# Edge counts kept in PSUM per 16 targets, 480-wide one-hots from two tensors, and four stages rearranged

## What is computed

```python
feat_all = einsum('ni,rhid->rnhd', x, conv_weights)      # layer 0: attention over 8 relations, 4 heads
h = segment_sum(alpha * feat_all[type8, src], dst)       # alpha: softmax of leaky_relu(el + er) per dst
agg = segment_sum(relu-MLP_r(x)[src], dst)               # layer 1: 2 relations, gates, 3 small products
aggr = segment_sum(relu(x @ Wp + bp)[src], dst) / cnt    # layer 2: SAGE, twice
out = rows of xt gathered by dst, weighted by softmax over heads    # layer 3: first 1875 edges only
```

## Time and profile before

| | us |
|---|---|
| runs | 2119.39, 2126.85, 2128.66 |
| median | 2126.85 |
| the profiled execution, its own time | 2116.86 |
| its span, first to last instruction | 2115.1 |
[...]
| PE busy | 1475.9 |
| DVE busy | 1249.3 |
| ACT busy | 666.2 |
| POOL busy | 543.2 |

### The profile page before, as it was taken

One profiled execution on the slowest core, in us unless ns is written; L12 is line 12 of the kernel. 1 busy time (PEld: TensorE's weight loads), 2 busy tenths in 40 slices (PEclk: granted clock), 3 DMA queues, 4 the chain that ended last, 5 costly groups with the idle time before them and its releaser, 6 DMA issues.

```text
span 2115.1 us, 20437 instructions
## 1 busy us (share of the span) xinstructions
PE 1475.9 (70%) x5426; PEld 764.4 (36%) x5426; DVE 1249.3 (59%) x2926; ACT 666.2 (31%) x1118; POOL 543.2 (26%) x517
## 2 busy tenths in 40 slices
PE   6598988677766565304777775989976589889630
PEld 3254654111111111103555554544433254644520
DVE  5221222889998888687666676520036677576705
ACT  1024764677665555200000000357732110010010
POOL 0003774677777777300000000000000000000031
PEclk9797556555555555555999998989987579999865
DMA  5924664465565565502677772000000000000021
GB/s 197 64 106 152 195 208 132 128 196 182 182 197 185 191 195 184 159 0 91 192 207 207 204 208 86 1 22 1 1 1 0 30 1 1 1 1 2 10 65 49
DMA packets 98133, 223.84 MB, mean 106 GB/s; under 512 B 32984, under 2 KB 57476, under 8 KB 97540
## 3 DMA queue, kind: packets, MB, share of 16 engines
q1 hardware_dynamic: 74084, 158.00, 23.8%
q0 software_dynamic: 23968, 64.77, 11.6%
HBM read 140.09 MB, written 82.63 MB: 105 GB/s over the span
## 4 chain that ended last, share of the span: by engine, by line
PE 48%; DVE 21%; issue 12%; POOL 12%; DMA 3%; DVEq 2%; ACT 1%; SPq 1%; POOLq 0%; ACTq 0%
PE bank L1580 14%; POOL arena L497 10%; PE bank L1519 10%; PE bank L1397 5%; DVE adjacency L936 5%; PE bank L1430 3%; PE bank L1416 3%; DVE arena L1193 2%; DVE arena L1001 2%; PE bank L1646 2%; PE bank L1564 1%; PE bank L1643 1%; SPq L363 1%; PE bank L1548 1%; DVE arena L930 1%
## 5 line engine op out<-in xcount | busy, mean ns | idle before, releaser
L497 POOL DMA_INDIRECT arena<-feat_table,arena x469 | 506.8, 1081 | 300.0 <-issue 138.3
L1467 PE MATMUL bank<-arena 128*128 128x480 f16 x586 | 319.6, 565 | 176.2 <-DVE arena L930 125.2
L565 ACT ACTIVATE arena<-bank 128x480 uint16<-128x480 f32 x586 | 307.9, 586 | 85.1 <-PE bank L1467 82.7
L505 POOL DMA_INDIRECT arena<-al_table,edge_ends x15 | 14.1, 942 | 1168.0 <-DMA al_table<-arena 1163.7
L1580 PE MATMUL bank<-arena 128*128 128x472 f16 x1440 | 294.3, 368 | 9.9 <-DVE arena L1151 5.9
L1519 PE MATMUL bank<-arena 128*128 x966 | 225.9, 387 | 83.1 <-issue 83.0
L936 DVE TENSOR_TENSOR adjacency<-adjacency,arena 128x480 uint16 x586 | 234.9, 401 | 23.4 <-ACT arena L565 16.7
L1519 PEld LDWEIGHTS bank<-arena 128*128 128x128 f32 x966 | 180.1, 191 | 129.2 <-issue 106.7
L1467 PEld LDWEIGHTS bank<-arena 128*128 128x128 f16 x586 | 60.7, 104 | 435.2 <-DVE arena L930 272.0
L930 DVE TENSOR_SCALAR arena<-iota,arena 128x480 f16<-128x480 f16 x586 | 201.5, 344 | 0.0
L1580 PEld LDWEIGHTS bank<-arena 128*128 128x128 bf16 x1440 | 142.6, 99 | 161.7 <-issue 15.5
(11 more groups left out here) (273 smaller groups left out, 1565.7 us busy)
## 6 DMA issues: line engine op xcount, KB each, us to landing
edge_rows<-arena SPq DMA_DIRECT2D x67, 910.0 KB, 4.1
arena<-edge_rows SPq DMA_DIRECT2D x117, 520.0 KB, 4.0
feat_table<-arena SPq DMA_DIRECT2D x60, 256.0 KB, 2.3
arena<-feat_table,arena POOLq DMA_INDIRECT x469
arena<-in_w SPq DMA_DIRECT2D x1, 2048.0 KB, 9.7
arena<-in_xT SPq DMA_DIRECT2D x1, 1920.0 KB, 18.5
arena<-in_x SPq DMA_DIRECT2D x1, 1792.0 KB
xt_table<-arena SPq DMA_DIRECT2D x3, 528.0 KB, 3.3
```

Of the source, the lines that this page charges most:

```text
L497: g.indirect_dma_start(out=SLOT[k][:, j, :], out_offset=None, in_=feat_t, in_offset=bass.IndirectOffsetOnAxis(ap=IE[:, GB * b + j:GB * b + ...
L565: a.activation(EV[st % AS].rearrange("p r k -> p (r k)"), PS[4 + st % 4][:, 0:R2 * KW], ACT.Copy)\
L1467: mm(PS[4 + st % 4][:, 0:R2 * KW], OHS[st % AS], OHK[st % AS], start=True, stop=True).then_inc(s["a_mm"], 1)
```

## The change

In the walk the two one-hots are made by `tensor_tensor` instead of `tensor_scalar`: the 480-wide one compares an fp16 iota with one fp32 key column that is repeated along the row (`column_of`), the 128-wide ones are made for eight steps at once (`rows_of`). PSUM counts are no longer started anew per step: four banks are cleared once, window w adds into bank w mod 4, and the matmul's output address comes from a register. ACT copies, in every step, the bank of the window before the current one straight into ADJ at that window's offset; both addresses come from registers, loaded 16 + 16 at a time from a 16-bit table, and each copy waits for the one before. As banks are never cleared again, a window's copy holds the sum of every fourth window up to it; 29 subtractions after the walk undo this. Zeroing of ADJ and DVE's adds are gone. PE may be three steps ahead of ACT, not four.

Around it: the row sums load their 16 + 16 offsets in one load per 16 steps; counts per target are made during the first aggregation, after ADJ's two relations are added together; layer 2 casts that sum on ACT; the gates' products of a chunk are issued before the x products of the chunk before it, bank by bank; the tail runs in four groups of up to four tiles, each with its own semaphore, with its own Exp, Sqrt and normalisation.

```diff
-GC_FIRST, GC_ER = 4, 14
+GC_FIRST, GC_ER, GC_LATE = 4, 14, 0
...
+RK = 2 * RG
+RKG = -(-RSTEPS // RK)
...
+        OHK = [AR[:, A_OH + k * KW:A_OH + (k + 1) * KW].bitcast(F16) for k in range(AS)]
+        OHS = [AR[:, o:o + AS * P // 2].bitcast(F16).rearrange("p (k e) -> p k e", e=P) for o in (A_OH + AS * KW, A_OHB)]
+        PBANK = AR[:, A_PBK:A_PBK + STRIDE // 2].bitcast(U16)
+        ETABf = AR[:, A_ETB:A_ETB + STRIDE].bitcast(U16)
+        ETAB = ETABf.rearrange("p (g two s) -> p g two s", two=2, s=16)
+        Z16 = AR[:, A_Z16:A_Z16 + KW].bitcast(F16)
...
-            def zero(lo, hi):
-                return a.activation(EARLY[:, lo:hi], ones[:, 0:1].to_broadcast([P, hi - lo]), ACT.Copy, scale=0.0)
...
-                zero(ZW * g, ZW * (g + 1))
                 if g >= GC_FIRST and g % 2 == 0:
                     collect((g - GC_FIRST) // 2)
-            act.wait_ge(s["er_mm"], NG)
-            zero(Z0, ZN).then_inc(s["a_add"], 1)
...
-            def a_evac(i, st):
-                act.wait_ge(s["a_mm"], i * AU + (st + 1))
-                a.activation(EV[st % AS].rearrange("p r k -> p (r k)"), PS[4 + st % 4][:, 0:R2 * KW], ACT.Copy)\
+            def a_evac(st, bank, off):
+                act.wait_ge(s["a_mm"], max(st, 1))
+                if st:
+                    act.wait_ge(s["a_ev"], st)
+                a.activation(ADJ[:, :, bass.ds(off, KW)], BANKS[:, bass.ds(bank, R2 * KW)].rearrange("p (r k) -> p r k", r=R2), ACT.Copy)\
                  .then_inc(s["a_ev"], 1)
-            for st in range(AS):
-                a_evac(0, st)
             got = GC_ER
-            for n in range(A_N):
-                for u in range(AU):
-                    a_evac(n, AS + u)
-                    due = GC_ER + (NGB - 1 - GC_ER) * (AU * n + u + 1) // (A_N * AU)
-                    while got < due:
-                        collect(got)
-                        got += 1
...
+            for st in range(STEPS):
+                if st % 16 == 0:
+                    both_ = offsets(ACTE, 2 * st, 32, KW * (WINS - 1), ETABf)
...
+                    offs = both_[16:32]
+                a_evac(st, banks[st % 16], offs[st % 16])
+                due = min(GC_ER + (NGB - 1 - GC_ER - GC_LATE) * (st + 1 - AS) // (STEPS - AS), NGB)
+                while got < due:
+                    collect(got)
+                    got += 1
+            a_evac(STEPS, 512 * (4 + (WINS - 1) % 4), KW * (WINS - 1))
...
+                    def cast(c):
+                        if c >= 2:
+                            act.wait_ge(s["chunk_used"], (R2 + v) * SH + c - 1)
+                        a.activation(chunk(CH2, c % 2, wide), ADJ[:, 0, :].rearrange("p (n s) -> p n s", s=SH)[:, :, c],
+                                     ACT.Copy).then_inc(s["chunk_ready"], 1)
                     for t in range(NT):
                         act.wait_ge(s["p_mm"], NT * v + t + 1)
                         message(t, t % 4, wide)
+                        if t in (6, 10):
+                            cast((t - 6) // 4)
+                    for c in range(2, SH):
+                        cast(c)
...
-            act.wait_ge(s["s3_ready"], 1)
-            a.activation(S3[:, 0, :], S3[:, 0, :], ACT.Exp).then_inc(s["s3_exp"], 1)
-            ln_sqrt(4)
+            for q, (t0, t1) in enumerate(GROUPS):
+                act.wait_ge(s["s3_ready"], q + 1)
+                a.activation(S3[:, 0, H * t0:H * t1], S3[:, 0, H * t0:H * t1], ACT.Exp).then_inc(s["s3_exp"], 1)
+                act.wait_ge(s["var_ready"], 3 + q + 1)
+                a.activation(RS[:, t0:t1], MV[:, t0:t1, 1], ACT.Sqrt).then_inc(s["std_ready"], 1)
...
+            W1 = slice(0, 1)
+            v.memset(ETABf[W1], 0)
+            v.tensor_copy(WCUR[W1], WS[W1])
+            link(v.tensor_scalar(WPRE[W1], WS[W1], 3.0, None, ALU.add))
+            v.tensor_single_scalar(WCUR[W1], WCUR[W1], 3, ALU.bitwise_and)
+            link(v.tensor_single_scalar(WPRE[W1], WPRE[W1], 3, ALU.bitwise_and))
+            def by_16(j, values, m, b):
+                full = STEPS // 16
+                v.tensor_scalar(ETAB[W1, 0:full, j, :], values[W1, 0:16 * full].rearrange("p (g s) -> p g s", s=16), m, b, ALU.mult, ALU.add)
+                v.tensor_scalar(ETAB[W1, full, j, 0:STEPS - 16 * full], values[W1, 16 * full:STEPS], m, b, ALU.mult, ALU.add)
+            by_16(0, WPRE, 512.0, 2048.0)
+            link(v.tensor_scalar(WS[W1], WS[W1], -1.0, 0.0, ALU.add, ALU.max))
+            v.tensor_scalar(PBANK[W1, 0:STEPS], WCUR[W1], 512.0, 2048.0, ALU.mult, ALU.add)
+            v.memset(Z16, 0.0)
+            by_16(1, WS, float(KW), 0.0)
...
-            def onehots(st, lo, key):
-                v.tensor_scalar(OHS[st % AS], iota128[:, :], lo, None, ALU.is_equal)
-                v.tensor_scalar(OHK[st % AS], iota480[:, :], key, None, ALU.is_equal).then_inc(s["a_oh"], 1)
-            def add_step(i, st, off):
-                dve.wait_ge(s["a_ev"], i * AU + (st + 1))
-                dve.wait_ge(s["a_add"], i * AU + (st + 1))
-                dst = ADJ[:, :, bass.ds(off, KW)]
-                v.tensor_tensor(dst, dst, EV[st % AS], ALU.add).then_inc(s["a_add"], 1)
-            dve.wait_ge(s["a_add"], 1)
...
+            def rows_of(st, n, lo):
+                v.tensor_tensor(OHS[st // AS % 2][:, 0:n, :], iota128[:, :].rearrange("p (a j) -> p a j", a=1).to_broadcast([P, n, P]),
+                                lo.rearrange("p (s a) -> p s a", a=1).to_broadcast([P, n, P]), ALU.is_equal).then_inc(s["a_rows"], 1)
+            def column_of(st, key):
+                v.tensor_tensor(OHK[st % AS], iota480[:, :], key.to_broadcast([P, R2 * KW]), ALU.is_equal).then_inc(s["a_oh"], 1)
+            rows_of(0, AS, SLO[:, 0:AS])
             for st in range(AS):
-                onehots(st, *step_cols(st))
+                column_of(st, KEY[:, st:st + 1])
+            dve.wait_ge(s["et_mm"], SC)
             with dve.Fori(0, A_N) as i:
-                offs = offsets(DVE, i * AU, AU, KW * (WINS - 1))
                 dve.wait_ge(s["a_oh"], i * AU + AS)
                 v.tensor_copy(SK, SLO_KEY[:, :, bass.ds(i * AU + AS, AU)]).then_inc(s["turn_cols"], 1)
                 dve.wait_ge(s["turn_cols"], i + 1)
                 for u in range(AU):
-                    add_step(i, u, offs[u])
-                    onehots(AS + u, SK[:, 0, u:u + 1], SK[:, 1, u:u + 1])
...
+                    dve.wait_ge(s["a_mm"], i * AU + (u + 1))
+                    if u % AS == 0:
+                        rows_of(AS + u, AS, SK[:, 0, u:u + AS])
+                    column_of(AS + u, SK[:, 1, u:u + 1])
+            for st in range(AS + A_N * AU, STEPS):
+                dve.wait_ge(s["a_mm"], st - AS + 1)
+                if st % AS == 0:
+                    rows_of(st, STEPS - st, SLO[:, st:STEPS])
+                column_of(st, KEY[:, st:st + 1])
+            dve.wait_ge(s["a_ev"], STEPS + 1)
+            for lo in range((WINS - 1) // 4 * 4 * KW, 0, -4 * KW):
+                n = min(4 * KW, WINS * KW - lo)
+                link(v.tensor_tensor(ADJ[:, :, lo:lo + n], ADJ[:, :, lo:lo + n], ADJ[:, :, lo - 4 * KW:lo - 4 * KW + n], ALU.subtract))
...
+            dve.wait_ge(s["chunk_ready"], SH)
+            link(v.tensor_tensor(ADJ[:, 0, :], ADJ[:, 0, :], ADJ[:, 1, :], ALU.add))
+            link(v.tensor_reduce(CNTX, ADJ[:, 0, :].rearrange("p (n s) -> p n s", s=SH), AX.X, ALU.add))
+            dve.wait_ge(s["chunk_used"], R2 * SH)
+            v.tensor_copy(CNTS, CNTX).then_inc(s["cnt_red"], 1)
...
-                n0, n1 = CQ * c, min(CQ * (c + 1), NW)
-                v.tensor_reduce(CNTS[:, n0:n1], ADJ[:, :, SH * n0:SH * n1].rearrange("p r (n s) -> p n r s", s=SH), AX.XY, ALU.add)\
-                 .then_inc(s["cnt_red"], 1)
...
-            def both(u, c, wide):
-                if c >= 2:
-                    dve.wait_ge(s["chunk_used"], base + u * SH + c - 1)
-                a0, a1 = (ADJ[:, r, :].rearrange("p (n s) -> p n s", s=SH)[:, :, c] for r in range(R2))
-                v.tensor_tensor(chunk(CH2, c % 2, wide), a0, a1, ALU.add).then_inc(s["chunk_ready"], 1)
...
-                    for c in range(2):
-                        both(u, c, False)
...
+            for q, (t0, t1) in enumerate(GROUPS):
+                n = t1 - t0
+                dve.wait_ge(g3[q], 16 * 2 * n)
+                sc, m3 = a3(0, t0, t1), S3[:, 1, t0:t1]
+                flat = S3[:, 0, H * t0:H * t1]
+                link(v.tensor_tensor(sc, AG3[:, t0:t1, :], G3[:, t0:t1, D + H:D + 2 * H], ALU.add))
+                link(v.scalar_tensor_tensor(flat, flat, 0.01, flat, ALU.mult, ALU.max))
+                link(v.tensor_reduce(m3, sc, AX.X, ALU.max))
+                v.tensor_tensor(sc, sc, wide(m3, n), ALU.subtract).then_inc(s["s3_ready"], 1)
+                dve.wait_ge(s["s3_exp"], q + 1)
...
+                for t in range(t0, t1):
+                    ins = v.bn_stats(ST[:, t, :], X[:, t, :])
+                link(ins)
+                for t in range(t0, t1):
```

(52 more changed lines are left out.)

128 lines of the change are left out of this document (55 added, 73 removed).

## The result

The changed kernel takes 2477.8 us in the median of 4 runs (2476.6 to 2481.3), the kernel before 2127.8 in runs beside them (4, 2119.4 to 2144.0): 1.164 times as long, with an interval of 1.157 to 1.171. The forecast, 2035, and its range, 1960 to 2130, missed it; the time is that of rival 1 (2390) and 88 us more. The profiled execution has a span of 2474.8 us.

A forecast was written before the change was run, and what follows sets the result against it. The walk, 500 of 2115 us, was held bound by gathers and adds ending close together. Terms +23 - 50 + 1 - 50 + 0 - 16 = -92 gave 2025 us profiled, 2035 against the median; range 1960 to 2130.

The forecast's parts named there:

- rival 1: Register loads priced per value, 7.7 us per 32: walk 803 us, row sums gain nothing, 2390 us in all; chance 0.16.
- By count and width of the load the first is nearest and I take 2.10: ACT's load of 32 half-words in the walk: 2.10 us, with bounds about 1.1 and 7.7.
- The one-hots of one tensor are what slows it: Walk's gathers on POOL: one-tensor one-hots slow them to 1108 ns; expected near 0.95 us after the change.
- this gain is not on the path as long as ACT sets the pace: Walk: faster gathers shorten nothing, since ACT's stream, 498 us in all, is later than the gathers.
- ACT's step: Walk: each self-linked evacuation on ACT takes 0.735 us, bounds 0.60 and 0.85.
- The 29 subtractions: New on DVE behind the walk: 1.19 us each, 35 us in all, on the path.
- The counts: Add and reductions moved beside PE's first aggregation: 15 and 30 us, hidden; a final copy on the path, +1.
- The gates: Reductions gone and products issued a chunk ahead: stage of about 90 us, -50 in the sum.
- SAGE messages: Two strided adds leave DVE, two casts on ACT come between messages: 0, plus or minus 6 us.
- tail: Last stage, done by groups of four tiles: ends 16 us earlier, -16.
- The row sums: One load per 16 steps: 8 steps in 4.35 us instead of 5.2, -50, bounds 0 and -90.
- rivals 2 to 4: Dear ACT link, 2110 us (0.17); cheap small loads and quick ACT, 1970 (0.15); later gains small, 2105 (0.12).

The follow-up runs named there:

- after: The changed kernel, unaltered: 2477.8 us in the median, 1.164 times the kernel before.
- b_half: The kernel before with DVE's 32 offsets per 32 steps held as 16-bit values instead of words: 2283.6 us beside 2255.6.
- w_small: The changed kernel with all tables as words, the walk's loads 8 words per 8 steps on PE and per 4 steps on ACT: 2029.9 us, ratio 0.953.
- before: The kernel before the change, unaltered: 2127.8 us in the median.
- w_all: The changed kernel with all three register tables as 32-bit words: 2109.0 us, ratio 0.933 to the kernel before.
- w_all_again: The changed kernel with all three register tables as 32-bit words, run a second time: 2114.5 us.
- rows_pairs: The changed kernel with the row sums' loads again in pairs of 8 half-words per 8 steps: 2438.8 us.
- w_scalar: The changed kernel with all tables as words and the 480-wide one-hots by the one-tensor operation again: ratio 0.962 to the kernel before.
- s_scalar: w_small with the 480-wide one-hots by the one-tensor operation again: 1968.4 us, ratio 0.916 to the kernel before.
- w_walk: The changed kernel with the walk's ACT and PE tables as 32-bit words, the row sums' table unchanged: 2289.0 us, ratio 1.016 to the kernel before.
- w_pe8: w_all with PE's banks in the walk loaded 8 words per 8 steps instead of 32 per 32: 2036.6 us, ratio 0.957.
- before_again: The kernel before, unchanged, profiled on another chip: 2253.6 us.

## Why the prediction was wrong

**The step that failed** is "By count and width of the load the first is nearest and I take 2.10". The load of 32 half-words takes 6.75 us on ACT and 7.53 on PE; the upper bound, 32 times 0.24 = 7.7, was the right price. The three rows held the answer: 32 words in 2.10 and 20 words in 1.37 lie on one line (66 to 69 ns each), and the only 16-bit row, 8 in 1.92, lies far off it. I weighed the number of values; what differed was the type. "time does not go with the number of registers alone" is true and speaks for a price by type, not for 2.10. The ends lay 5.6 us apart with 37 and 48 loads behind them, and 0.16 for the upper one was too little.

**Rival 1** had the mechanism and the walk: 803 us against 807, though of unlike parts (a load on ACT adds 6.6 us in the mean and not 7.2, PE's 6.8 and not 5.5). It erred in "the row sums gain nothing": they lost 101 us, since one load of 7.53 us outlasted the 4 us of queued matmuls (PE stood 3.8 us, and the clock of the stage was 0.75), where the same time in pieces of 1.92 us did not (PE stood 1.4 us, clock 1.00). Its price per value held for 16 bits (211 to 266 ns in the median) and not for words (61 to 75 ns).

**A second step failed behind the first**: "The one-hots of one tensor are what slows it", with "gathers near 0.95" once they are gone. Beside two-tensor one-hots they take 1.24 us, more than the 1.108 of before. With 0.30 us of issue, 346 of them need 533 us, more than the 498 of ACT's stream, so "this gain is not on the path as long as ACT sets the pace" failed with it. With words, and PE's eight at a time, the walk is then 549 us and not 498. The earlier trace rows held the warning: 314.6 us busy and 82.9 of issue are 397.5 of 400 us, so POOL had no slack in the kernel before either. That the two-tensor form would leave the gathers alone was my estimate, from four gathers of 985 ns beside adds alone; no run shows it, and the 1.24 us stands against it. Of the two 480-wide forms it was the one-tensor form, 344 ns in the earlier trace rows, beside which the gathers were delayed least (1.02 and 1.04 us in the two versions that have it). What a gather and a DVE operation contend for is shown by no run.

**Right, by their own runs or traces**: ACT's step, 0.757 for 0.735. The 29 subtractions, 34 us for 35:

```profile
L990 DVE TENSOR_TENSOR adjacency<-adjacency x29: 659/1158/1159, 1172.3 to 1205.2; 128x1920 uint16<-128x1920 uint16 x28, 128x960 uint16<-128x960 uint16 x1
```

The counts, 44.6 us beside PE, over at 1947 where PE ends at 1980, and 1.1 us of copy:

```profile
1902.73 14.91 DVE L1207 TENSOR_TENSOR adjacency<-adjacency 128x28320 uint16<-128x28320 uint16 x1 [69.73 <-ACT arena L634]
1917.67 29.65 DVE L1208 TENSOR_REDUCE arena<-adjacency 128x1888 f32<-128x28320 uint16 x1
```

The gates, 84 us for 90: the -50 of the sum was an estimate that no run shows as such; in its place the stage went from 138 to 84 us, with a granted clock of 0.92 where it was 0.73. SAGE messages 0; tail -20 for -16. The row sums with word loads, -74 for -50: 7.8 us per 16 steps and not 8.7, since behind a load of 2.13 us PE stood for 0.2 to 1.0 us. That the version with words and 8-word loads takes 2036.6 us, all but the forecast, is chance: its walk is 50 us over its term, the row sums are 25 under theirs and the rest 13, and the 10 us between a profiled execution and the median did not appear.

The rivals 2 to 4 did not decide: the link was not dear (0.757 us per evacuation), small loads were not cheap at 16 bits (6.75 us for 32 values), the later gains came in full.

## What to carry to other kernels

When a resource is bounded by two rows of different type, ask what the type does before what the count does, and give the far bound its due where it is multiplied by dozens. Keep tables from which registers are loaded as 32-bit words (32 in 1.97 us on ACT here, where 32 half-words took 6.75), and cut loads so small that each hides under the work that is already queued (0.55 us for 8 words, under an evacuation of 0.57): 16-bit tables saved some 5 KB of a partition and, with PE's loads of 32 values where 8 would do, cost 434 us on one chip (2470.7 against 2036.6). When a faster path frees an engine, look at once for the stream that has no slack left, here POOL's gathers, and at what the new operation does to it (1.24 us per gather where it was 1.108).

## What the runs showed of the hardware

- A load of registers took 0.21 us (ACT, in `after`), 0.22 to 0.28 (DVE, in `b_half`) and 0.235 (PE, in `after`) per 16-bit value, and 0.061 to 0.075 per 32-bit word: 8 in 0.55 to 0.60 (`w_small`), 20 in 1.37 (`before`), 32 in 1.97 (ACT) and 2.13 (PE, both in `w_all`). Its engine issued nothing meanwhile, and what was queued ran on: in `after` PE's load lasted from 1493.88 to 1501.41, the matmuls ran until 1497.9, and the next came at 1501.69. Some loads in the walk took longer at either width: 9 of ACT's 37 in `after` by 1.4 to 1.6 us, and the longest in `w_all_again`, of words, by 1.9 us (3.88 instead of 1.97); that is open.
- Behind a stand of 3.8 us PE's matmuls ran at the lower clock for about 5 us (`after`: 12 of them 0.43 us apart at 0.50 of full speed, then 0.22 at 0.98; the stage 0.75); behind 1.4 us they did not (`before` and `rows_pairs`: 1.00).
- A gather's time on POOL went with DVE's work: 0.95 us where DVE was idle (67 gathers in `before`, 190 in `after`), 1.02 and 1.04 beside one-tensor (`w_scalar`, `s_scalar`), 1.24 beside two-tensor 480-wide one-hots (`w_walk`, `w_pe8`), and 1.108 in the kernel before, where one-tensor one-hots and adds keep DVE busiest (355 of 400 us).
- On two of the chips the same kernel took 117 to 128 us longer (2245 and 2256 us for 2128), on the one where it was profiled (`before_again`) all ahead of the scans. Its sequencer instructions of 0.70 us are part of that at most: ahead of the walk, 60 us longer, only some 10 are over 0.3 us. The rest is open.
